# Own buffers for chunk 7's split rows, ones of the keys copied by transfers, chunk 1's statistics in front of two weights' split, chunk 2's residual rows behind its attended rows

## The reference

```python
x = x + 0.5 * ffn(layernorm(x), w_router, b_router, w_experts, b_experts)
x = x + attn(layernorm(x), w_qkv, w_proj, b_proj, ln_gamma, ln_beta)
x = x + 0.5 * ffn(layernorm(x), ...)            # the same weights
```

## Time and profile before

| | us |
|---|---|
| median of 3 runs | 996.08 |
| lowest, highest | 994.55, 997.16 |
| the profiled execution: its time | 996.42 |
| its span, first to last instruction | 994.7 |
| mean granted TensorE clock | 0.990 |

### The profile page before, as it was taken

The page is one execution under the profiler, slowest core; times in us unless marked ns, Lnnn a source line. Parts: engine busy times, 40 slices in busy tenths (PEclk is TensorE's granted clock), DMA queues, the critical chain, the costliest instruction groups (busy, mean ns, idle before and its releaser), DMA issues.

```text
span 994.7 us, 17662 instructions
## 1 busy us (share of the span) xinstructions
PE 955.4 (96%) x5602; PEld 567.4 (57%) x5602; DVE 830.3 (83%) x2445; ACT 511.0 (51%) x1053; POOL 264.3 (27%) x288
## 2 busy tenths in 40 slices
PE   6899998999998899999999999999998999999998
PEld 4678886777776233333333333333344777777776
DVE  6677777688686899999999999999768788888775
ACT  4235423424315677777777777777775333232310
POOL 1012204202205222222221221222343553434210
PEclk9999999999999899999999999999999999999999
DMA  6201121101023433223222322233320111110001
GB/s 225 90 1 64 51 77 65 37 28 64 34 63 97 128 77 77 78 73 75 61 76 61 72 66 66 72 78 77 92 61 13 43 65 64 64 56 21 8 22 42
DMA packets 55109, 64.32 MB, mean 65 GB/s; under 512 B 13824, under 2 KB 37360, under 8 KB 55024
## 3 DMA queue, kind: packets, MB, share of 16 engines
q1 hardware_dynamic: 54432, 62.47, 22.1%
q10 hardware_dynamic: 592, 0.80, 0.2%
HBM read 41.30 MB, written 21.23 MB: 63 GB/s over the span
## 4 chain that ended last, share of the span: by engine, by line
PE 85%; DVE 7%; issue 3%; ACT 2%; POOL 2%; DMA 1%; DVEq 0%; SPq 0%; ACTq 0%; POOLq 0%
PE bank L362 39%; PE bank L1611 14%; PE bank L1435 13%; PE bank L1593 13%; PE bank L857 2%; PE bank L354 2%; POOL a_part L496 1%; DVE bank L1462 1%; ACT b_probs L1570 1%; DMA v_all<-L_ffn_w_experts 1%; DVE a_acc L1081 1%; PE bank L803 1%; DVE c_acc L1081 1%; POOL b_ks L1408 1%; DVE a_st L317 1%
## 5 line engine op out<-in xcount | busy, mean ns | idle before, releaser
L1570 ACT ACTIVATE b_probs<-bank 128x512 f32<-128x512 f32 (+1 forms) x608 | 302.9, 587 | 114.8 <-PE bank L1593 114.4
L1462 DVE CUSTOM_DVE_ANT_0 bank<-bank,b_below 128x384 f32<-128x384 f32 (+3 forms) x512 | 235.2, 515 | 10.8 <-PE bank L1435 9.3
L1435 PE MATMUL bank<-b_ks,b_qs 96*128 96x512 bf16 (+3 forms) x768 | 222.8, 331 | 10.1 <-DVE b_neg L1462 4.1
L1593 PE MATMUL bank<-b_qs,b_ks 99*128 99x512 bf16 (+3 forms) x768 | 214.9, 331 | 4.5 <-ACT b_probs L1570 4.3
L362 PE MATMUL bank<-we,a_xt 128*128 128x512 f32 x768 | 194.2, 405 | 0.9 <-DVE a_acc L1081 0.9
L362 PE MATMUL bank<-we,c_xt 128*128 128x512 f32 x768 | 186.2, 398 | 0.9 <-DVE c_acc L1081 0.8
L1541 POOL TENSOR_SCALAR_AFFINE_SELECT b_probs<-b_probs 128x512 f32<-128x512 f32 x128 | 83.9, 656 | 323.9 <-ACT b_probs L1570 323.9
L1466 DVE TENSOR_REDUCE b_neg<-bank 128x1 f32<-128x512 f32 x256 | 161.2, 679 | 2.7 <-PE bank L1435 1.2
L362 PEld LDWEIGHTS bank<-we,c_xt 128*128 128x128 f32 x768 | 142.3, 188 | 33.5 <-DVE c_acc L1081 1.9
L362 PEld LDWEIGHTS bank<-we,a_xt 128*128 128x128 f32 x768 | 142.4, 191 | 28.9 <-DVE a_acc L1081 1.5
L1611 PE MATMUL bank<-b_probs,b_vs 128*32 128x512 f32 (+3 forms) x1536 | 156.6, 502 | 0.9 <-POOL b_probs L1541 0.9
(11 more groups left out here) (136 smaller groups left out, 891.1 us busy)
## 6 DMA issues: line engine op xcount, KB each, us to landing
b_qs<-q_parts SPq DMA_DIRECT2D x96, 128.0 KB, 3.0
b_ks<-k_parts SPq DMA_DIRECT2D x96, 128.0 KB, 3.0
q_parts<-a_part SPq DMA_DIRECT2D x16, 384.0 KB, 2.6
k_parts<-a_part SPq DMA_DIRECT2D x16, 384.0 KB, 2.7
att_num<-b_oev SPq DMA_DIRECT2D x64, 64.0 KB, 2.2
c_num<-att_num SPq DMA_DIRECT2D x8, 512.0 KB
c_rec<-att_rec SPq DMA_DIRECT2D x16, 256.0 KB
out<-xs SPq DMA_DIRECT2D x7, 512.0 KB, 3.3
```

Of the source, the lines that this page charges most:

```text
L1435: last = nc.tensor.matmul(ms[bank][:, a * width:(a + 1) * width], qs[g.u][0:ROWS, c, i * P:(i + 1) * P], ks[g.u][0:ROWS, c, lo:lo + width] ...
L1462: last = dve.tensor_tensor_reduce(part, part, below[:, CH - width:CH], -1.0, 3.0e38, ALU.add, ALU.min, dst[:, a, :])
L1570: act.activation(probs[b % 4][:, heads[0]:heads[0] + hp, 0:width], es[exp_bank(g, unit)][:, 0:hp * width].rearrange("p (h w) -> p h w", w= ...
L1593: last = nc.tensor.matmul(es[exp_bank(g, unit)][:, a * width:(a + 1) * width], ks[g.u][:, c, j * P:(j + 1) * P], qs[g.u][:, c, first_q:fir ...
```

## The change

- Chunk 7's split rows get buffers of their own, `last_rows`, laid over `ybias` and `acc`. `split2` of chunk 7 waits for chunk 7's last `x` instead of the products of chunk 6.
- The ones of `ks[1]` and `ks[2]` are no longer filled by POOL but copied from `ks[0]` by SP (`copy_ones`). The fill of `vs[1]` stays on POOL, behind chunk 7's third parts. The first exponential product of groups 1 and 2 waits for the copies and that fill.
- In chunk 7's slot DVE does `scale2` ahead of the read of position 38. `values` of chunk 7 is cut in two pairs with positions 42 and 43 between them; 44 to 46 follow the second. The last remainder of chunk 7 (`qk_rests`, 3) moves behind two reads of the attention.
- In the lead DVE does chunk 1's statistics (`norm(1)`, `scale(1)`) ahead of the low halves of two weights. ACT copies chunk 0's first biases ahead of `norm(1)`, and in slot 0 chunk 1's mask ahead of `spread(2)`. PE does two banks of tile 1 ahead of chunk 1's transposition.
- The first unit of chunk 4 (behind bank 0 of tile 0) moves back one bank, and chunk 5 gets a unit behind its bank 0.
- Chunk 2's residual rows are computed behind `attended(2, 0, 1)`. POOL adds their bias in the last group, and shifts chunk 2's rows only once chunk 0's mask is ready.

```diff
-EARLY = {NCH - 4: range(8), NCH - 3: range(1, 8), NCH - 2: range(8), NCH - 1: (*range(8), *range(9, 16))}
+EARLY = {NCH - 4: range(1, 8), NCH - 3: range(8), NCH - 2: range(8), NCH - 1: (*range(8), *range(9, 16))}
-FIRST = (38, 39, 40, 42, 47)
+FIRST = (38, 39, 40, 42, 44, 47)
...
+        last_rows = [nc.alloc_sbuf_tensor_at(f"{tag}_last{n}", [P, DK, CH], F32R, offset=ybias_at + 4 * n * DK * CH)
+                     for n in range(2)]
+    def rows2(m):
+        return last_rows if isinstance(m, int) and m == NCH - 1 else xt2r
# SP, slot of chunk 7 and the one behind it
                     a.load_part(sp, Group(0, 1), False)
+                    a.copy_ones(sp, 1)
                     a.place_maxima(sp, Group(0, 0))
+                if isinstance(c, int) and c == NCH:
+                    sp.wait_ge(q.v_bank, at(2 * NCH))
+                    a.copy_ones(sp, 2)
# POOL, slot
+                if exists(c - 1):
+                    low_parts(c - 1)
                 if isinstance(c, int) and c == NCH:
-                    pool.wait_ge(q.qk_lo, at(4 * (NCH - 1)))
-                    pool.wait_ge(q.v_bank, at(2 * NCH))
-                    a.ones_keys(pool, 2, 4)
-                    a.ones_values(pool, 1, 5)
-                if isinstance(c, int) and c == NCH - 1:
-                    low_parts(c - 1, (0, 1))
-                    pool.wait_ge(q.qk_lo, at(4 * (c - 1) + 2))
-                    pool.wait_ge(q.ffn_bank, at(16 * NCH))
-                    a.ones_keys(pool, 1, 3)
-                    low_parts(c - 1, (2, 3))
-                elif exists(c - 1):
-                    low_parts(c - 1)
+                    pool.wait_ge(q.qk_lo, at(4 * NCH))
+                    a.ones_values(pool, 1, 3)
...
                 if (early, block) == (0, 4):
                     shift_x(1)
+                    add_bias(2)
             a.gpsimd(pool, lead)
-            add_bias(2)
+            pool.wait_ge(q.mask_ready, at(1))
             shift_x(2)
# ACT
         def split2(m):
             act.wait_ge(q.turned2, at(m + 1))
-            act.wait_ge(q.v_bank, at(2 * m))
-            act.wait_ge(q.qk_bank, at(4 * m))
+            if isinstance(m, int) and m == NCH - 1:
+                act.wait_ge(q.x_ready, at(TPC * NCH))
+            else:
+                act.wait_ge(q.v_bank, at(2 * m))
+                act.wait_ge(q.qk_bank, at(4 * m))
...
             spread(1)
+            bias_out(0, 0)
             norm(1)
# PE
         def queries_keys(m, c, which=range(4)):
+            if not isinstance(m, int) or m == 0:
+                pe.wait_ge(q.wqk_lo, 2)
...
                 experts(0, 0, 0, (3,))
-                pe.wait_ge(q.wqk_lo, 2)
+                experts(0, 0, 1, (0, 1))
...
-                values(c - 1)
-                if not exists(c):
+                if exists(c):
+                    values(c - 1)
+                else:
+                    values(c - 1, (0,))
                     a.first_scores(pe, FIRST[3], FIRST[4])
+                    values(c - 1, (1,))
+                    a.first_scores(pe, FIRST[4], FIRST[5])
                 queries_keys(c - 1, c)
# DVE
         def split2(m):
             dve.wait_ge(q.hi2_ready, at(m + 1))
-            dve.wait_ge(q.qk_bank, at(4 * m))
+            if not (isinstance(m, int) and m == NCH - 1):
+                dve.wait_ge(q.qk_bank, at(4 * m))
...
                 stats2(c)
+                scale2(c)
                 a.first_reads(dve, FIRST[0], FIRST[1])
-                scale2(c)
...
             elif first and exists(c - 1):
-                qk_rests(c - 1)
+                qk_rests(c - 1, (0, 1, 2))
+                s.last_rest = lambda: qk_rests(c - 1, (3,))
...
             ranks(0, 0)
+            norm(1)
+            scale(1)
             dve.wait_ge(q.wqk_hi, 1)
             dve.tensor_tensor(s.wqk[1][:], ...)
...
-            norm(1)
-            scale(1)
...
                     attended(2, 0, 1)
+                    dve.wait_ge(q.resid_bias, at(2))
+                    dve.sem_inc(q.apart, 1)
+                    scale_tiles(resid, xs_tile(2), s.ln2[:, tiles(2), :], q.resid_ready)
                     split_lo(0, 0)
...
                 if (early, block) == (0, 2):
-                    dve.wait_ge(q.resid_bias, at(2))
-                    dve.sem_inc(q.apart, 1)
-                    scale_tiles(resid, xs_tile(2), s.ln2[:, tiles(2), :], q.resid_ready)
                     ranks(0, 0)
# attention
+    def copy_ones(sp, u):
+        sp.wait_ge(vones, at(2))
+        sp.dma_start(ks[u][ROWS:MROWS, :, :], ks[0][ROWS:MROWS, :, :]).then_inc(ones_copied, 16)
...
+            if unit == 0 and g.n in (1, 2):
+                pe.wait_ge(ones_copied, at(16 * 2))
+                pe.wait_ge(vones, at(3))
...
-        pe.wait_ge(vones, at(5))
+        pe.wait_ge(vones, at(2))
...
                 max_read(dve, *entry)
+                if (g.n, at) == (0, 1):
+                    s.last_rest()
```

More of the change, by code:

```diff
@@ L667, in slot @@
         def slot(c, par, nth):
-            if exists(c):
+            begins = first and isinstance(c, int) and c == 0
+            if exists(c) and not begins:
                 bias_out(c, 0)
@@ L683, in slot @@
                 residual(c + 3)
+            if begins:
+                mask_out(c + 1, 1 - par)
             if exists(c + 2):
                 spread(c + 2)
-            if exists(c + 1):
+            if exists(c + 1) and not begins:
                 mask_out(c + 1, 1 - par)
@@ L831, in turn2, with values @@
             transpose_chunk(pt, xh2).then_inc(q.turned2, 1)
-        def values(m):
+        def values(m, pairs=(0, 1)):
             pe.wait_ge(q.lo2_ready, at(m + 1))
-            for pair in range(2):
+            for pair in pairs:
                 for i in range(2):
                     t = 2 * pair + i
-                    last = pair_product(pt[pair][:, i * D:(i + 1) * D], s.wv, slice(0, D), xt2r, slice(t * P, (t + 1) * P),
+                    last = pair_product(pt[pair][:, i * D:(i + 1) * D], s.wv, slice(0, D), rows2(m), slice(t * P, (t + 1) * P),
                                         False)
@@ L878, in slot @@
             if exists(c):
-                experts(c, par, 1)
+                experts(c, par, 1, (2, 3) if first and isinstance(c, int) and c == 0 else range(4))
             spread_units = first and isinstance(c, int) and c in EARLY
@@ L1326, in attention @@
     a.os = os_ = s.banks[6:8]
-    consts, vones = sem("consts"), sem("vones")
+    consts, vones, ones_copied = sem("consts"), sem("vones"), sem("ones_copied")
     loaded = [sem(f"loaded{u}") for u in range(3)]
```

14 lines of the change are left out of this document (9 added, 5 removed).

## The result

The changed kernel takes 985.33 us (median of 4 runs, 984.34 to 986.08) beside 995.93 of the kernel before on the same chip: ratio 0.9895, 95% interval 0.9882 to 0.9907. Two more sets of runs gave medians of 983.26 (ratio 0.9878, 0.9861 to 0.9894) and 984.53 (0.9895, 0.9879 to 0.9912). Forecast 985.0, range 981.5 to 990.5. The profiled execution took 985.25, span 983.5.

What follows compares the result with a forecast made beforehand. PE, busy 96% of the span, was taken as the bound, so only its waits pay. Gains 2.7 + 1.7 + 4.9 + 1.8 = 11.1 take 996.42 to 985.3, with the median 0.3 lower at 985.0; range 981.5 to 990.5.

Steps and rivals of the forecast that it cites:

- Lead: Start of the kernel, chunk 1's statistics first: shorter PE wait and no clock fall, gain 2.7, bounds 0.9 to 3.1.
- The lead is swallowed: Rival, chunk 1's start: PE waits for DVE's sums anyway, so 2.7 is lost, 987.7; chance 0.05.
- Early scores: First scores of chunks 4 and 5 moved: chunk 4 gains 2.9, chunk 5 loses 1.2; gain 1.7, bounds 0.5 to 2.5.
- Handover: From feed-forward to attention, chunk 7 to group 2's first score: earlier values, queries and reads; gain 4.9, bounds 1.9 to 5.4.
- that rival: Group 2's load: the moved last remainder holds its store and the load as long as before, 988.5; chance 0.08.
- the clock falls all the same: Rival, start and chunk 7's passage to attention: half clock still follows, taking 1.3 and 1.93, 988.3; chance 0.12.
- Back: From attention to the second feed-forward part: mask ready earlier, PE's 1.86 wait gone; gain 1.8, bounds 0 to 1.9.
- loses 0.1: Tile 1 of the second feed-forward part: PE, there at 773.3, waits 0.1 for tile 0's first sums at 773.4.
- The rule's 0.4: Last group's selection at 760.79: by the port-lock rule one 0.43 ranks step could hold it, making the sum 0.4 less.
- Attention: The regular attention, PE and DVE both nearly full, passes an earlier start on unchanged; no gain of its own.
- Copies of ones: Rival, groups 1 and 2: SP's copies land late and hold exponential products; decides if the second lands after 340; chance 0.03.
- It does not do what it says: Rival, whole change: some wait is only passed to the next one and under 3 us remain, 994; chance 0.05.

Runs made afterwards that it cites:

- the early scores undone: Changed kernel with chunk 4's scores again from its first bank on and chunk 5's from its second: 985.91 us, ratio 0.9900.
- the run with the remainder in order: Changed kernel with chunk 7's last remainder back ahead of DVE's first attention reads: 985.09 us, ratio 0.9888.
- that of the ones: Changed kernel with the keys' ones filled by POOL again at the old places instead of copied by SP: 986.39 us, ratio 0.9903.
- handover undone: Changed kernel with old split-row buffers, POOL's ones fills, scores behind both value pairs and last remainder in order: 990.31 us, ratio 0.9944.
- own buffers undone: Changed kernel with only chunk 7's split rows back in the old shared buffers, behind the old waits: 989.18 us, ratio 0.9920.
- two edits that removed 1.5 and 3.4 us of waits: Each on the changed kernel: POOL readies `below` ahead of chunk 2's third parts, 983.62 us; ACT copies chunks 4 to 7's first bias earlier, 982.46 us.

## Why the prediction was right

**Lead.** Foretold 2.7; the segment gives 2.67 in one pair of profiles and 2.8 in the other. Each link held: wait 1.67 (1.7), transposes 1.03 (1.0), 24 products 6.00 (5.8). "The lead is swallowed" is false: chunk 4's bias product is 2.3 earlier (151.75 against 154.07), after a first one that was 0.35 later.

**Early scores.** Foretold 2.9 less 1.2; measured 3.17 less 1.04 (and 0.06 in chunk 6), 2.1 net. The slot of chunk 4 lost 0.3 more than foretold: its first score came 4.64 behind the bias product, 1.66 later than in the pattern that was taken over, and 0.63 of it was made up behind the score, where 0.3 was taken. Part of the 3.17 is clock, which fell behind the 2.84 us wait of before and not behind the 1.50 (see the early scores undone).

**Handover.** Foretold 4.9, measured 3.9 in the first profile and 5.4 in the second, that is the upper bound, which held if the load bound nothing. Values came 1.6 earlier (1.5), queries 2.4 (2.0), the third remainder 3.35 (49.46 instead of 52.81 after the bias product; 3.1). Two things were off and hid each other. The last issue of the load moved by 4.4, not 3.5: the order on the queue cost nothing, and moving the fourth remainder did not hold the store but brought it forward, by 1.0, as the run with the remainder in order shows; 330.81 plus the 3.0 of the earlier trace rows is 333.8, 2.5 ahead of the read. And the clock fell at 320 all the same in the first profile, which left DVE's 2.06 us wait where 1.93 was to go. With the clock up, the rows land at about 334.0 (last issue at 331.00) and are read at 334.80: the load would be next, but does not rule. So that rival is false, and "the clock falls all the same" is true in one of the three profiled executions at this place, and in none of them in the lead.

**Back.** Foretold 1.8, bounds 0 to 1.9. The mask wait is gone and projection to first bias product is 4.35 instead of 6.38, 2.0 less. But at tile 1 PE's timeline of the kernel before had been

```profile
774.13 1.03 PE L354 MATMUL bank<-ident,c_xh 128*128 128x128 f32 x8
774.92 5.82 PE L362 MATMUL bank<-we,c_xt 128*128 128x512 f32 x24
```

so the transposes overlapped the next products by 0.24, and now PE stands 0.42 before these for DVE's first sums: from the last projection to tile 1's first product it is 11.61 instead of 13.00, 1.4 in all, the 1.4 of the fit. The step that was mis-sized is "loses 0.1". DVE's sums were through 11.55 after the projection, which is 773.47 on the times of before and near my 773.4. But PE was through with its transposes at 11.19, 0.2 earlier than my 773.3, since more than the wait had gone in front, and I left out the 0.24 of overlap that such a wait breaks. The fixed point was right: DVE's first sum comes 10.68 after the last projection, before 10.67, since it follows the transfer of the last group.

The ports: with chunk 2's rows back in place, DVE's two steps ended 0.29 behind the additions of POOL that they met (above). The selection does the same to a step that starts behind it. In the changed kernel the step of 751.15 took 0.74 instead of 0.42 and ended at 751.89, 0.28 behind the selection of 750.93. In the kernel before, the step next to the very selection that the prediction names (760.79, 0.63 long, to 761.42) took 0.87 and ended 0.27 behind it, and further up one selection of POOL met a step of DVE that had started first. DVE's timeline, then POOL's:

```profile
753.72 1.23 DVE L1188 TENSOR_TENSOR c_yg<-c_yn,gamma 128x1024 f32<-128x1024 f32 x1
...
760.82 0.87 DVE L1038 TENSOR_TENSOR c_gt<-c_logits 128x256 f32<-128x256 f32 x1
```

```profile
754.34 1.11 POOL L1541 TENSOR_SCALAR_AFFINE_SELECT b_probs<-b_probs 128x512 f32<-128x512 f32 x1 [11.37 <-ACT b_probs L1570]
```

Here DVE's step kept its 1.23, to 754.95, and the selection took 1.11 instead of 0.63 to 0.64. So whichever of the two starts first holds the other. The prediction read the row of 760.79 as "not held"; that selection had started first, and DVE was the one that was held, by 0.45. The trace agrees with the Trainium skill (SBUF — State Buffer, "SBUF: two separate sides"): a VectorE instruction with two inputs in SBUF contends with a GpSimd instruction that reads SBUF, and the other side is blocked for the whole of it. The rule's 0.4 was right in kind and too large, because only the end of a step was left: the selection of 750.93 met the last 0.19 of the step of 750.70 and took 0.68. PE waited 1.06 for it, before 0.90; some 0.05 of the 0.16 is the longer selection, and the rest is that it started 0.87 instead of 0.76 behind PE's products before it. A step of any size can be held so: the one at 753.29 works on 128 by 4 elements (0.15 to 0.16 when POOL is quiet) and took 1.94, to end at 755.23 with POOL's addition at 755.20.

**Attention.** Taken to pass an earlier start on unchanged. From group 2's first score to the last projection it is 417.3 before and 415.8 after, 415.6 and 415.0 in the other two profiles. The 1.5 was not foretold, and the traces put it down to the clock: the kernel before had half clock twice inside the attention, from 716 to 720 and from 747 to 750, the changed kernel once in each of its first two profiles (737 to 741, 735 to 738) and not at all in the third. A window of before, where PE is busy throughout:

```profile
717.00:718.00 1.00, 1.00 (x12) 0.21 (x4) 0.00 (x0) 0.00 (x0) 0.32 (x1) 0.50 0.47 129
```

With it the gains of the first profile add up to the difference of the spans, 11.2: lead 2.67, chunks 4 to 7 2.07, chunk 7 to group 2 3.87, attention 1.55, last projection to the end 1.39, less 0.35 by which the first bias product came later. So it is in part luck that the sum, 985.3 for the profiled execution, met its 985.25: the handover and the back gave 1.4 less than foretold in this pair of profiles, and the early scores' 0.4 more and the clock in the attention, put at nothing, made up for it.

**Clock.** The sum had 1.3 of clock in the lead and 1.9 in the handover, 3.2 of 11.1. The fit gives 2.6 of 11.3. The two sizes are near each other, but they don't count the same falls: those of the sum are the lead's and the handover's alone, the fit's hold chunk 4's slot and the attention as well. The clock is also why most of the later expectations missed on the median. For own buffers the expectation lay 2.5 below what was measured and for the whole handover 1.1 below, for the others of one part 0.7 to 1.5 above. Most segments came out as written; own buffers' did not (queries 3.4 later instead of 1.2 to 1.6, with the clock at 0.50), nor did that of the ones (1.4 instead of 2 to 2.6). The expectations added a part's segment to 985.3, one draw of a number that lies anywhere from 982.8 to 986.2.

**Copies of ones.** Both were issued by 311.3 and neither was waited for. "It does not do what it says" is false: no wait was passed on whole.

What stays open: why the same wait is followed by half clock in one execution and not in another, and why the clock falls between 320 and 335 in seven of the fourteen profiles, for 3 to 10 us, among them one of three of the changed kernel. All three kernels with the wait for the old split rows (before, handover undone, own buffers undone) have it, and of the eleven profiles without this wait four do. I found nothing in the traces ahead of the fall that tells the cases apart, and no run here was made for it.

## What to carry to other kernels

Cost a wait of PE twice: by its length, and by what it can do to the clock behind it. Here an own buffer that removed a 2.2 us wait was worth some 1.7 in the one execution whose clock stayed up and over 5 in the three where it fell; half of the rest was a fall that came elsewhere without this wait, so it can't all be promised to the buffer. To judge one part of a change of 1 to 3 us, compare a segment of the trace between two fixed instructions, or fit the time with the granted clock beside it; the median of four or five runs alone did not resolve it. And ask first whether the next engine is close behind: two edits that removed 1.5 and 3.4 us of waits shortened their segments by 0.8 each, since DVE was late by nearly as much (seven waits for it, 3.5 in all, in the second).

## What was not expected of the hardware

Executions of one program have mean granted clocks from 0.994 to 1.000 and times 3.4 us apart; the three that were profiled (0.995, 0.998, 1.000) have the same waits ahead of the place where the clock fell in one of them to 0.50 (1.2 GHz instead of 2.4). A 2.2 us wait was followed by full clock in the earlier trace rows and by half clock in the run without own buffers. And a vector instruction of 128 by 4 elements can take 1.94 us instead of 0.16, if it meets an addition on POOL: a small step is held to the end of a large one. Held steps of DVE with 128 by 256 elements ended 0.27 to 0.29 us behind POOL's instruction, beside additions and selections alike, and this one of 128 by 4 ended 0.03 behind its addition.
